# Flamingo gated block with eight routed experts: slot 0 gathered whole and turned by TensorE, half of expert 1 loaded early, each scatter placed between the halves of a gather, and VectorE's turning of rows moved behind its weight splits

## The reference

```python
# 1. cross attention stand-in: both operands fake-quantised to 8 bits, one matmul
x = x + tanh(g_xattn[0]) * (fake_quant(layernorm(x)) @ fake_quant(ctx))
# 2. mixture of experts over y = layernorm(x)
logits = y @ W_gate + b_gate                          # 8 experts
_, top_idx = top_k(logits, 2)
y_all = relu(einsum('bsd,edh->bseh', y, W_e) + b_e)   # W_e: 8 x 1024 x 1024
x = x + tanh(g_ffn[0]) * mean(y_all[the two of top_idx])
```

## Time and profile before

| | |
|---|---|
| median of three runs | 373.47 us |
| the profiled execution's own time | 372.75 us |
| its span | 371.0 us |
| TensorE (PE) busy | 320.1 us, 86% |
| VectorE (DVE) busy | 253.9 us, 68% |
| GpSimd (POOL) busy | 198.1 us, 53% |
| ScalarE (ACT) busy | 129.2 us, 35% |
| mean granted TensorE clock | 0.934 |
| DMA | 81.46 MB, mean 220 GB/s |

### The profile page before, as it was taken

One profiled execution on the slowest core, in us unless ns is written; L12 is line 12 of the kernel. 1 busy time (PEld: TensorE's weight loads), 2 busy tenths in 40 slices (PEclk: granted clock), 3 DMA queues, 4 the chain that ended last, 5 costly groups with the idle time before them and its releaser, 6 DMA issues.

```text
span 371.0 us, 6691 instructions
## 1 busy us (share of the span) xinstructions
PE 320.1 (86%) x1602; PEld 241.0 (65%) x1612; DVE 253.9 (68%) x348; ACT 129.2 (35%) x109; POOL 198.1 (53%) x208
## 2 busy tenths in 40 slices
PE   4669887999668798599997999999999999999950
PEld 1224364577543586488885888887888888788840
DVE  3898997878975719639887593587553955695430
ACT  3865876453100263108361711360116310811100
POOL 4552451300426860467782686576566856766661
PEclk9699999999758899699999899999999999999985
DMA  6999385412262595957999799579656896714553
GB/s 233 414 408 391 144 335 233 170 57 85 112 259 72 188 406 215 324 112 168 368 342 408 182 307 324 116 189 409 171 113 160 255 357 137 175 46 99 119 121 57
DMA packets 20012, 81.46 MB, mean 220 GB/s; under 512 B 4256, under 2 KB 4256, under 8 KB 15904
## 3 DMA queue, kind: packets, MB, share of 16 engines
q1 hardware_dynamic: 12272, 57.71, 40.6%
q0 software_dynamic: 7584, 23.60, 27.8%
q10 hardware_dynamic: 144, 0.01, 0.0%
HBM read 62.43 MB, written 18.87 MB: 219 GB/s over the span
## 4 chain that ended last, share of the span: by engine, by line
PE 37%; DVE 25%; issue 11%; POOL 11%; DMA 6%; POOLq 3%; ACT 3%; DVEq 2%; ACTq 0%
PE ps L1222 30%; POOL y_rows L458 7%; DVE w_lo L835 5%; DMA y_rows<-y_scratch,gidx 4%; DVE st L695 4%; PE ps L1028 3%; POOLq L287 2%; POOL gidx L454 2%; DVE xt L759 2%; DMA par<-in_small_dram 2%; DVEq L287 1%; ACT w_hi L630 1%; PE ps_s L1080 1%; DVE onehot L820 1%; DVE res L990 1%
## 5 line engine op out<-in xcount | busy, mean ns | idle before, releaser
L458 POOL DMA_INDIRECT y_rows<-y_scratch,gidx x88 | 110.8, 1259 | 37.7 <-issue 19.8
L1222 PE MATMUL ps<-w_hi,yT_hi 128*128 x320 | 101.2, 398 | 13.4 <-DVE yT_lo L829 13.0
L1222 PE MATMUL ps<-w_hi,yT_lo 128*128 x320 | 100.9, 397 | 0.0
L1222 PE MATMUL ps<-w_lo,yT_hi 128*128 x320 | 100.6, 396 | 0.0
L616 ACT ACTIVATE yT_hi<-ps_y 128x1024 fp32r<-128x1024 f32 x21 | 21.5, 1025 | 168.7 <-DVE ps_y L958 104.4
L1222 PEld LDWEIGHTS ps<-w_hi,yT_hi 128*128 128x128 f32 x320 | 61.2, 192 | 28.6 <-issue 16.0
L835 DVE TENSOR_TENSOR w_lo<-stage,w_hi 128x2048 f32 (+1 forms) x32 | 71.1, 2274 | 0.1
L1222 PEld LDWEIGHTS ps<-w_hi,yT_lo 128*128 128x128 f32 x320 | 61.6, 192 | 13.1
L1222 PEld LDWEIGHTS ps<-w_lo,yT_hi 128*128 128x128 f32 x320 | 61.2, 191 | 12.9
L486 POOL DMA_INDIRECT out_dram<-res,sidx x20 | 32.6, 1632 | 51.9 <-DVE res L992 34.4
L630 ACT ACTIVATE w_hi<-stage 128x2048 f32 x28 | 51.9, 1909 | 13.5 <-DMA stage<-in_L_ffn_W_e_dram 13.5
(11 more groups left out here) (161 smaller groups left out, 259.4 us busy)
## 6 DMA issues: line engine op xcount, KB each, us to landing
stage<-in_L_ffn_W_e_dram SPq DMA_DIRECT2D x32, 1024.0 KB, 7.3
stage<-in_ctx_dram SPq DMA_DIRECT2D x16, 512.0 KB, 11.4
xt<-in_x_dram SPq DMA_DIRECT2D x8, 512.0 KB, 11.1
y_scratch<-y SPq DMA_DIRECT2D x8, 512.0 KB, 3.4
bias<-in_L_ffn_b_e_dram SPq DMA_DIRECT2D x8, 512.0 KB, 4.6
out_dram<-xt SPq DMA_DIRECT2D x6, 512.0 KB, 3.0
y_rows<-y_scratch,gidx POOLq DMA_INDIRECT x88
out_dram<-xt POOLq DMA_DIRECT2D x2, 512.0 KB, 7.8
```

What stands on the lines that cost most here:

```text
L458: pool.indirect_dma_start(out=y_rows[q][:, b * QD:(b + 1) * QD], out_offset=None, in_=y_quarters[:, :], in_offset=bass.IndirectOffsetOnAxi ...
L1222: last = pe.matmul(ps[q][:, h * 512:(h + 1) * 512], lhs[q][:, k, :], w[:, bass.ds(woff + k * D + h * 512, 512)], start=(k == 0 and lhs is ...
```

## The change

1. The host no longer reorders `W_e`. Tile k of the weights now holds rows 8p + k, so the rows of y are turned with a stride: block k takes every eighth float. VectorE's transpose reads with that stride.
2. Slot 0 is gathered by one indirect DMA of whole rows, as soon as `idx` is ready. `idx` is computed two small instructions earlier. TensorE turns slot 0 with eight transposes. There are 2 + 14 + 6 fill matmuls where there were 4 + 30.
3. Chunks 0 and 1 of expert 1 are loaded between the stores of y, chunks 2 and 3 behind the biases; SyncE waits no more for gathers.
4. In GpSimd's step the gather of slot k+3 is cut in two. Quarters 1 and 2 go before the wait for slot k's result, quarters 3 and 4 after the scatter.
5. In VectorE's step the turn of slot k+2 goes behind the low parts of the weights. Before the loop likewise.

```diff
-    w_t = W_e.rearrange("e p k h -> p e k h")
+    w_t = W_e.rearrange("e (p k) h -> p e k h", p=P)
 ...  # SyncE
-            for i in range(TPB, NT):
-                store_y(i)
+            store_y(4)
+            store_y(5)
+            for c in range(2):
+                sp.wait_ge(s_lo, c + 1)
+                load_w1(c)
+            store_y(6)
+            store_y(7)
 ...
-            for q in range(2):
-                sp.wait_ge(s_g[q], 16 * NQ)
-            with sp.Fori(1, E) as n:
+            for c in range(2, NCH):
+                sp.wait_ge(s_lo, c + 1)
+                load_w1(c)
+            with sp.Fori(2, E) as n:
 ...  # GpSimd
+            pool.wait_ge(s_idx, 1)
+            pool.indirect_dma_start(out=y_rows[0][:, :], out_offset=None, in_=y_dram[:, :],
+                                    in_offset=bass.IndirectOffsetOnAxis(ap=idx[:, 0:1], axis=0)).then_inc(s_g[0], 16)
             pool.wait_ge(s_qidx, 1)
-            for b in range(NQ):
-                pool.indirect_dma_start(out=y_rows[0][:, b * QD:(b + 1) * QD], ...)
             pool.wait_ge(s_col, 1)
-            gather(1, 1, 1)
+            pick_rows(1, 1, 1)
+            gather_quarters(1, 0, NQ)
             pool.wait_ge(s_tp, 1)
-            gather(2, 0, 2)
+            pick_rows(2, 0, 2)
+            gather_quarters(0, 0, NQ)
 ...
                 pool.wait_ge(s_tp, slot + 2)
-                gather(slot + 3, 1 - q, slot * 2 + 3)
+                pick_rows(slot + 3, 1 - q, slot * 2 + 3)
+                gather_quarters(1 - q, 0, NQ // 2)
 ...              # wait for slot k's result, scatter
+                gather_quarters(1 - q, NQ // 2, NQ)
 ...  # VectorE
-                              y_rows[q][:, :].rearrange("p (b k r) -> p k b r", b=NQ, k=KT)).then_inc(s_tp, 1)
-            turn_rows(0, 1)
+                              y_rows[q][:, :].rearrange("p (b c k) -> p k b c", b=NQ, k=KT)).then_inc(s_tp, 1)
 ...
                 evacuate_lo(1 - q)
-                dve.wait_ge(s_el, slot + 2)
-                turn_rows(q, turn + 2)
                 with dve.If(nxt > 0):
                     for c in range(NCH):
                         split_lo(...)
+                dve.wait_ge(s_el, slot + 2)
+                turn_rows(q, turn + 1 + q)
 ...  # TensorE
-            keep_clock(30, ps[0][:, 512:1024])
+            keep_clock(14, ps[0][:, 512:1024])
+            pe.wait_ge(s_g[0], 16)
+            for k in range(KT):
+                last = pe.transpose(ps_y[:, k, :], y_rows[0][:, :].rearrange("m (p k) -> m k p", k=KT)[:, k, :],
+                                    ident_f[:, :])
+            last.then_inc(s_tp, 1)
+            keep_clock(6, ps[0][:, 512:1024])
```

More of the change, by code:

```diff
@@ L306, in load_w0, with load_w1 @@
                 sp.dma_start(stage[:, CK * c:CK * (c + 1), :], w_t[:, 0, CK * c:CK * (c + 1), :]).then_inc(s_w[c], 16)
+            def load_w1(c):
+                sp.dma_start(stage[:, CK * c:CK * (c + 1), :], w_t[:, 1, CK * c:CK * (c + 1), :]).then_inc(s_w[c], 16)
             def load_bias(e):
@@ L362, in _ @@
                                  ).then_inc(s_w[c], 16)
[L363 to L371, removed]
+                sp.wait_ge(s_post, entry(sp, BAS - 1, n, MAX_SLOTS, lo=1))
+                settle(sp)
+                for q in range(2):
+                    with sp.If((n & 1) == q):
+                        sp.dma_start(bias[:, q * D:(q + 1) * D],
+                                     b_e[bass.ds(n, 1), :].rearrange("a d -> (a d)").partition_broadcast(P)
+                                     ).then_inc(s_bias[q], 16)
                 sp.nop()
@@ L449, in _, with pick_rows @@
                 pool.dma_start(out_t[i], xt[:, i, :]).then_inc(s_sc, 16)
-            def gather(slot, q, step):
+            def pick_rows(slot, q, step):
                 col = entry(pool, COL, slot, (E + 1) * SPE - 1)
@@ L456, in gather, with gather_quarters @@
                 settle(pool)
-                for b in range(NQ):
+            def gather_quarters(q, first, end):
+                for b in range(first, end):
                     pool.indirect_dma_start(out=y_rows[q][:, b * QD:(b + 1) * QD], out_offset=None, in_=y_quarters[:, :],
@@ L492, in _ @@
             pool.wait_ge(s_sc, n * 16 + 32)
-            pool.wait_ge(s_g[0], ((n + 4) >> 1) * (16 * NQ))
+            pool.wait_ge(s_g[0], ((n + 2) >> 1) * (16 * NQ) + 16)
             pool.wait_ge(s_g[1], ((n + 3) >> 1) * (16 * NQ))
@@ L616, in evacuate_hi @@
                 act.activation(yT_hi[q][:, :, :], ps_y[:, :, :], ACT.Copy).then_inc(s_eh, 1)
-            act.wait_ge(s_tab, 1)
             act.wait_ge(s_tp, 1)
             evacuate_hi(0, 0)
+            act.wait_ge(s_tab, 1)
             act.wait_ge(s_oi, 16 * (NT - 2))
@@ L915, in _ @@
             count, base_, rest = cnt[:, 0, :], cnt[:, 1, :], cnt[:, 2, :]
+            dve.wait_ge(s_abs, 1)
+            dve.tensor_scalar(idx[:, :], tok_abs[:, :], 1.0, -1.0, ALU.max, ALU.add).then_inc(s_idx, 1)
             link(dve.tensor_scalar(cnt8[:, :], ps_c[:, NT * E:(NT + 1) * E], 1.0 / P, 0.494, ALU.mult, ALU.add))
             link(dve.tensor_scalar(count[:, 0:E], cnt8[:, :], 1.0, None, ALU.max))
-            dve.wait_ge(s_abs, 1)
-            dve.tensor_scalar(idx[:, :], tok_abs[:, :], 1.0, -1.0, ALU.max, ALU.add).then_inc(s_idx, 1)
             dve.wait_ge(s_spread, 1)
@@ L952, in _, with turn_rows @@
             dve.wait_ge(s_tab, 1)
-            def turn_rows(q, n_gathers):
-                dve.wait_ge(s_g[q], n_gathers * (16 * NQ))
+            def turn_rows(q, quartered):
+                dve.wait_ge(s_g[q], quartered * (16 * NQ) + (16 if q == 0 else 0))
                 settle(dve)
                 dve.transpose(ps_y[:, :, :].rearrange("p k (b r) -> p k b r", b=NQ),
-                              y_rows[q][:, :].rearrange("p (b k r) -> p k b r", b=NQ, k=KT)).then_inc(s_tp, 1)
-            turn_rows(0, 1)
+                              y_rows[q][:, :].rearrange("p (b c k) -> p k b c", b=NQ, k=KT)).then_inc(s_tp, 1)
             dve.wait_ge(s_eh, 1)
@@ L1199, in _ @@
             place_rows(2)
-            keep_clock(4, ps[0][:, 512:1024])
+            keep_clock(2, ps[0][:, 512:1024])
             pe.wait_ge(s_abs, 1)
```

3 lines of the change are left out of this document (removed).

## The result

The change made the kernel slower: median 437.4 us of four runs (436.44 to 438.72) against 374.22 beside it (369.62 to 375.26); ratio 1.174, 95% interval 1.165 to 1.184. The forecast was 422 us, in a range of 396 to 437: the direction and the loop were right, but the median is 15 us above the forecast and just outside the range. The profiled execution took 438.72 us, its span 437.0.

A forecast was written before the change was run, and what follows sets the result against it. TensorE set 10.88 us a slot; the change adds a longer loop through the late gather. Slot 0 complete 139.7, slots 1 to 19 272.3, tail 8.6: span 420.6, with 1.75 around it 422 us, range 396 to 437.

The forecast's parts named there:

- a ring through scatter, late quarters, turn and result: In the slot loop: slot k+1's result waits for a gather that starts after slot k's result; 13.15 us against 10.88.
- the predicted signs: VectorE waiting 60 to 100 us before turns, results every 13 us, TensorE waiting for yT_lo, granted clock 0.5 repeatedly.
- the fourth quarter's flight among weight loads: In steps that split weights: the last late quarter lands 6.0 us after its start, bounded by 2.8 and 8.2.
- their high bounds: Whole kernel: every predicted term at its upper limit gives 440 us; all at their low limits give 395.
- slot 0 complete: End of VectorE's work on the first slot's result: predicted at 139.7 us, where it was 151.06.
- slots 1 to 19: From slot 0's result to slot 19's: ordinary and split steps together predicted at 272.3 us.
- tail: From slot 19's result to the span's end: 0.85 us to the scatter, then 7.8; 8.6 instead of 11.2.
- The head: Before the loop: earlier idx, one whole-row gather and fewer fills start slot 0 at 118.9, 4.3 us earlier.
- ordinary steps: Twelve loop steps without weight splits, at 13.15 us each, bounds 12.4 and 13.6; 157.8 us in all.
- Steps with splits: Slots 3, 4, 6, 9, 13 at 17.3 us each (bounds 14.0 and 19), 86.5 in all; slot 16 14.0.
- Rival 1: Loop without contention: late quarters pass the weight chunks and reads cost a little less; 398 us; chance 0.25.
- rival 4: TensorE, idle 2 to 6 us every slot, stays at 1.2 GHz for most of each; 435 us and more; chance 0.08.

The follow-up runs named there:

- The first run: Changed kernel with all four quarters of slot k+3 issued ahead of the wait for slot k's result, the scatter last: 365.81 us, ratio 0.989.
- the head alone: Kernel before with only parts 1 and 2 of the change (strided rows, whole-row gather for slot 0, eight transposes, fewer fills): 376.01 us, ratio 1.014.
- part 4 alone: Kernel before with only the gather cut in two, quarters 3 and 4 behind the scatter: 463.25 us, ratio 1.252.

## Why the prediction was right in kind and short in size

The mechanism was the one predicted: a ring through scatter, late quarters, turn and result that takes longer than TensorE's 10.88 us a slot. The first run shows it by removal, and the predicted signs were there: waits in front of the turn 97.0 us (60 to 100), waits for yT_lo in 14 slots, the lower clock after stops. What failed is the sum. It put slot 1's gather and turn, which stand ahead of expert 1's splits, at no delay, and they cost 3.8 us; it took the 7.8 us behind the last scatter as fixed, and they became 12.6; and it gave the fourth quarter's flight among weight loads 6.0 us, where 7.5 was measured. The prediction's own terms at their high bounds came to 440, but its range ended at 437 and so left no room for such misses. The span missed by 16.4 us (437.0 against 420.6):

| term | predicted | measured | miss |
|---|---|---|---|
| slot 0 complete | 139.7 | 145.83 | +6.1 |
| slots 1 to 19 | 272.3 | 277.69 | +5.4 |
| tail | 8.6 | 13.48 | +4.9 |

**The head.** idx was ready 1.7 us later than predicted (111.27, not 109.55). The granted clock from 60 to 65 us was 0.66 in this execution and 1.00 in the run with the scatter last; other executions with the same head had idx at 109.5, and the unaltered head has both values too, so this is scatter between runs. The whole-row gather let TensorE begin 4.45 us after its start (3.8 predicted for the landing); the fills ended at 116.41 and were no hindrance. Slot 0 began 9.3 us behind idx, as predicted (109.55 to 118.9). The other 4.4 us come behind that. The prediction had VectorE split expert 1's weights from 127.4; it began at 132.87, and of these 5.5 us only 1.7 are idx. VectorE was done with expert 0's splits at 124.58 and then stood idle for 3.07 us before slot 1's turn (127.64), which itself took 2.12 us instead of 1.26. ScalarE's high parts and VectorE's low parts of expert 1 stand behind that turn, and slot 0's result behind them; the strided turn of slot 2 adds the last 0.7.

Most of the 3.07 us comes from two parts of the change that meet. The kernel with the head alone has the same slow fourth quarter, but no load in flight beside it:

```profile
120.25 2.90 POOL L464 DMA_INDIRECT y_rows<-y_scratch,gidx  x1 [0.30 <-issue]
...
125.04 2.14 DVE L966 STREAM_TRANSPOSE ps_y<-y_rows 128x1024 f32<-128x1024 f32 x1 [0.51 <-issue]
```

There the loads start at 125.42 and VectorE idles 0.51 us. With the early loads alone the quarter is issued in 0.95 us, before the loads, and VectorE does not idle at all. With both, the late quarter meets chunks 2 and 3 (122.40), and it is 3.07. The prediction had costed the early loads at nothing and did not look at this quarter.

The Trainium skill, page "SBUF — State Buffer", section "Who interferes with whom", says that a VectorE instruction with two SBUF inputs contends with GpSimd's reads; the split is one, and a quarter's issue took 2.91 us beside it instead of 0.95. The same section infers that such an instruction leaves GpSimd's making of descriptors alone. The traces do not bear that out: with no load in flight, too, the issue took 2.90. The trace of before had shown the effect (1.89 against 0.94), and I used it in the loop but not in the head.

**The loop, ordinary steps.** Predicted 13.15, measured a mean of 13.28 in the twelve (12.8 to 14.7). That is two misses that cancel. From scatter to fourth quarter 3.22 (3.2 predicted), from result to scatter 0.85 (as predicted); but result to turn is 8.1, not 7.25, since I let the quarter land 6.2 us behind the scatter's start and it takes 7.1. I had read the scatters' median landing, 6.3, as the moment for the quarter too. The quarter came 0.8 after that. Then turn to result takes 3.0, not 3.8: the stops for VectorE's sequencer were 22.0 us in 9 before and are 16.2 in 18 now, none above 1.1. The strided turn fills this time, 2.13 instead of 1.26.

**Steps with splits.** Predicted 17.3; measured 17.5, 18.4, 18.3, 17.8 and 18.1, in sum 90.1 against 86.5. The mis-sized term is the fourth quarter's flight among weight loads, 6.0 predicted, 7.5 measured (177.41 to 185.07 less the handover); the turn starts 12.5 to 13.1 us behind the result, not 11.4, and the shorter stretch from turn to result takes back 0.8 of it. Slot 1 took 13.4, not 14.0. Slot 16, without loads, took 14.8, not 14.0: there the strided turn's 0.87 us does show, where I had taken the low bound of 0 to 2.5. The Trainium skill, page "SBUF — State Buffer", section "Door 1: The DMA port swizzle", says that each access that crosses to a new 16-byte line pays a penalty; the trace agrees in kind, with 2.13 us for the strided turn instead of 1.26.

**Rival 1,** quarters that slip between the weight packets, is refuted: by it the split steps would have taken 14.0. They came near that only with loads a sixteenth as long.

**The tail.** I took what stood behind the last scatter before, 7.8 us, as fixed; it was 12.6. The last DRAIN took 5.30 instead of 1.18 us, which is 4.1 of the 4.9, and it began 7.1 us behind the scatter's start instead of 6.4, which is the rest. The two late quarters now stand behind the last scatter too, and with part 4 alone it is 7.1 as well. Nothing in the trace of before told of the long drain. It goes with the whole-row gather: 5.18 to 5.30 us in all nine kernels run that have it, 1.10 to 1.18 in the seven that have not. Why is open.

**The clock** (rival 4) is not the cause. TensorE's busy time rose by 14 us, with stretches at the lower level behind stops, as before. This one follows the stop ahead of slot 2 (stretch, length, busy us, PEclk, DMA share, GB/s):

```profile
145.80:152.60 6.80, 4.98 (x12) 3.92 (x13) 1.25 (x2) 0.00 (x0) 4.47 (x5) 0.50 0.82 205
```

But it lies inside steps that VectorE sets: in no step of the loop did VectorE wait for TensorE before its result. All 16.2 us of its idle time there is "issue".

## What to carry to other kernels

Before an instruction is moved past a wait on an in-order engine, write down the ring that it closes: here two gathers of 1 us each, moved behind a scatter, tied slot k+3's rows to slot k's result and cost 93 us alone. A gather issued behind a scatter in the same queue pays for the scatter, and moving one of two out from behind it gave back only 17 of 72 us. Parts that meet must be costed together: the slow quarter and the early loads idled VectorE for 0.5 and 0 us alone, and for 3.1 together. The same change carried two good ideas, early loads and waits placed behind work that is due anyway, and they only showed once each part was run by itself.

## What the runs showed of the hardware that was not expected

- After one indirect gather of 128 rows of 4 KB, GpSimd's final DRAIN took 5.2 to 5.3 us instead of 1.18, 245 to 320 us later. With quarters instead, or in the kernel before, it is 1.18; three further small gathers leave it at 5.18.
- A quarter behind a full accumulating scatter lets VectorE start 4.09 us after its start, behind a scatter of a quarter of the bytes 2.92 us.
- VectorE's 32 x 32 transpose of 128 x 1024 floats takes 2.02 to 2.21 us when it reads every eighth float, 1.26 when it reads 32 in a row.
- GpSimd's issue of an indirect DMA takes 0.95 us alone and mostly 1.7 to 3.1 us beside VectorE's two-input splits (128 x 2048 floats), with weight loads in flight or without. Where the strided turn stood right ahead of the splits (the strided turn alone, the head alone) three took 4.8, 5.3 and 8.65 us.
- A gather of 128 x 256 floats behind a scatter is usable 4.1 us after its start in an ordinary step and 7.7 us after it with 1 MB weight loads issued beside it.
